# First experts' rows added to nodes in DRAM by accumulating scatters, in a GNN and MoE kernel on one core

## What is computed

```python
x = x + L0_gnn(layernorm(x), src, dst, ...)        # attention over edges
# L0_ffn: 8 experts, each node goes to its best 2; an expert takes 187 nodes
xf = layernorm(x)
probs = softmax(xf @ gate_w.T + gate_b)
topw, topi = top_k(probs, 2)
sel_w, sel_idx = top_k(wm.T, cap)                  # per expert: the nodes it takes, their weights
h = gelu(einsum('ecd,edh->ech', xf[sel_idx], w1) + b1)
out = einsum('ech,ehd->ecd', h, w2) + b2
of = zeros((T, D)).at[sel_idx].add(out * sel_w)
x = x + of
x = x + L1_gnn(layernorm(x), edge_attr_4, edge_attr_8, ...)   # messages, summed per node
x = x + L1_ffn(layernorm(x), ...)                  # two banks of 8 experts
```

## Time and profile before

| | us |
|---|---|
| median of three runs | 1875.65 (1869.82 to 1876.59) |
| the profiled execution | 1875.17 |
| its span, first to last instruction | 1873.40 |
| PE, DVE, ACT, POOL busy | 1594.3, 959.7, 701.4, 559.6 |
| first experts, first matmul of rows to last copy of a result | 867.23 to 1211.61 |
| opening of messages, first instruction to first gather | 1216.20 to 1267.03 |
| ACT's clear of 12 blocks | 1216.22 to 1221.54 |

### The profile page before, as it was taken

The page is one execution under the profiler, slowest core; times in us unless marked ns, Lnnn a source line. Parts: engine busy times, 40 slices in busy tenths (PEclk is TensorE's granted clock), DMA queues, the critical chain, the costliest instruction groups (busy, mean ns, idle before and its releaser), DMA issues. The chain is left out here.

```text
span 1873.4 us, 31644 instructions
## 1 busy us (share of the span) xinstructions
PE 1594.3 (85%) x9860; PEld 1167.9 (62%) x9860; DVE 959.7 (51%) x1950; ACT 701.4 (37%) x1610; POOL 559.6 (30%) x638
## 2 busy tenths in 40 slices
PE   1993077999999797897999999858999999898994
PEld 0551045888888455555999999844555555655662
DVE  8330098766766386361000000168999999542233
ACT  0230055555555133443211112154555555441331
POOL 6777601101010121151000000046555555133133
PEclk6997588999999898798999999968999999998997
DMA  9900011011000600557566552075555555619985
GB/s 290 312 11 6 6 43 23 13 23 22 12 11 1 149 12 1 220 142 249 198 229 238 218 196 99 18 216 165 156 158 158 156 156 150 215 37 287 353 268 183
DMA packets 131143, 252.87 MB, mean 135 GB/s; under 512 B 35344, under 2 KB 52596, under 8 KB 126572
## 3 DMA queue, kind: packets, MB, share of 16 engines
q1 hardware_dynamic: 91692, 171.81, 27.6%
q0 software_dynamic: 39360, 79.86, 14.6%
HBM read 196.03 MB, written 55.52 MB: 134 GB/s over the span
## 5 line engine op out<-in xcount | busy, mean ns | idle before, releaser
L1998 PE MATMUL acc<-prod,ohy 128*64 128x256 f32 x1056 | 249.1, 386 | 7.3 <-DVE prod L2116 7.3
L2042 ACT ACTIVATE ohy<-oh,RECS 128x64 f32<-128x64 f32 x704 | 187.0, 336 | 151.6 <-PE acc L1998 151.6
L1998 PEld LDWEIGHTS acc<-prod,ohy 128*64 128x64 f32 x1056 | 138.4, 138 | 131.9 <-issue 69.5
L1975 POOL DMA_INDIRECT rows<-up_dram,idx x176 | 167.0, 949 | 144.3 <-DVE prod L2116 101.2
L272 POOL DMA_INDIRECT rec_dram<-recs,pos x157 | 160.4, 1022 | 59.9 <-issue 48.9
L2001 PE MATMUL acc<-prod,ohy 128*64 128x256 f32 x704 | 177.3, 395 | 0.0
L1752 DVE TENSOR_SCALAR FT<-y_ps,b2T 128x188 f32<-128x188 f32 x32 | 13.2, 413 | 319.2 <-PE y_ps L1701 319.2
L1689 PE MATMUL hid_ps<-FT,W 128*128 128x188 f32 x1024 | 168.1, 326 | 0.7 <-ACT FT L1726 0.7
L2116 DVE TENSOR_TENSOR prod<-w_ps,rows 128x768 f32<-128x768 f32 x176 | 166.3, 945 | 0.0
L1689 PEld LDWEIGHTS hid_ps<-FT,W 128*128 128x128 f32 x1024 | 165.6, 192 | 0.9 <-issue 0.9
L1701 PE MATMUL y_ps<-hid,W 128*128 128x188 f32 x1024 | 164.5, 323 | 0.0
(11 more groups left out here) (380 smaller groups left out, 2638.2 us busy)
## 6 DMA issues: line engine op xcount, KB each, us to landing
W<-in_L_ffn_w SPq DMA_DIRECT2D x16, 4096.0 KB, 15.9
bankW_sp<-in_L_ffn_W_sp SPq DMA_DIRECT2D x2, 4096.0 KB, 23.9
xin<-zeros SPq DMA_DIRECT2D x31, 256.0 KB
h_dram<-h3e SPq DMA_DIRECT2D x22, 256.0 KB, 4.8
h<-h_dram SPq DMA_DIRECT2D x22, 256.0 KB
QF<-q_dram SPq DMA_DIRECT2D x20, 250.0 KB, 4.1
xin_sp<-zeros SPq DMA_DIRECT2D x17, 256.0 KB
xin_fq<-zeros SPq DMA_DIRECT2D x17, 256.0 KB
```

Of the source, the lines that this page charges most:

```text
L1975: pool.indirect_dma_start(out=rows[:, t, :], out_offset=None, in_=up_dram, in_offset=bass.IndirectOffsetOnAxis(ap=idx[:, par, t:t + 1], ax ...
L1998: upper = lambda m: nc.tensor.matmul(acc[0:HALFB, bank, :].rearrange("p (b c) -> p b c", c=MUL)[:, m:4:3 - m, :], ohs[:, 1 + m, :], pr[:, ...
L2042: last = nc.scalar.activation(ohy[:, t % OHY, i, :], oh[:, par, t, :], ACT.Copy, scale=RECS[:, bass.ds(BATCH * g + t, 1), 4 + i])
```

## The change

Every row that goes to an expert gets 8 more columns (EXTRA): its two weights, its two experts, and four times its node's number. A blank row carries zeros and a number past the 1250 nodes, a different one for each of 128 rows. X is stored to a new DRAM array, x_dense, during place_choices. Each expert's DVE part reads from its rows the node numbers (nodeI) and the weight that belongs to this expert, and weights the result as it copies it to ye. POOL then adds ye to the rows of x_dense by two scatters per expert, 94 rows each, in which the DMA adds to what stands there; each waits until the one before has landed. messages opens by loading X back from x_dense, tile by tile, on SP; gathers, additions, slot_out, yout0 and the wait before RECS are gone. POOL, not ACT, clears the 12 blocks of MSG. DVE's and POOL's loops over experts are written out.

```diff
+EXTRA = 8
+WIDE_ROW = DIM + EXTRA
...
-    xin0 = dram("xin0", (EXPERTS * ROWS0 + 2 * NODES, DIM))
-    yout0 = dram("yout0", (EXPERTS * ROWS0, DIM))
+    xin0 = dram("xin0", (EXPERTS * ROWS0 + 2 * NODES, WIDE_ROW))
+    x_dense = dram("x_dense", (NODES + 128, DIM))
...
+                        zeros_in += fill_zeros(sp, x_dense[NODES:NODES + 128, :], zeroed)
...
+                        nc.gpsimd.iota(zeros[:, DIM + 4:WIDE_ROW], pattern=[[0, 4]], base=NODES, channel_multiplier=1,
+                                       allow_small_or_imprecise_dtypes=True)
+                        nc.gpsimd.memset(zeros[:, 0:DIM + 4], 0.0).then_inc(consts, 1)
...
                         for b in range(ECHUNKS):
                             store_hidden(sp, b)
+                            if b < TILES:
+                                for p0, p1 in TILE_PARTS:
+                                    sp.dma_start(x_dense[P * b + p0:P * b + p1, :], X[p0:p1, b, :]).then_inc(x_stored, 16)
                         all_stored(sp)
+                        sp.wait_ge(x_stored, 32 * TILES)
...
+                        nc.gpsimd.iota(N[:, :, DIM + 4:WIDE_ROW], pattern=[[P, TILES], [0, 4]], base=0, channel_multiplier=1,
+                                       allow_small_or_imprecise_dtypes=True).then_inc(tagged, 1)
                         pool.wait_ge(bases_ready, 1)
+                        pool.wait_ge(tagged, 3)
...
+                        nc.vector.tensor_copy(N[:, :, DIM:DIM + 2], best[:, :, 0:2]).then_inc(tagged, 1)
+                        nc.vector.tensor_copy(N[:, :, DIM + 2:DIM + 4], idxF[:]).then_inc(tagged, 1)
...
-                        step(nc.vector.tensor_reduce(rank[:], parts[:], X_AXIS, ALU.add))
-                        step(nc.vector.tensor_scalar(keep[:], rank[:], CAP0 - 0.5, None, ALU.is_lt))
-                        step(nc.vector.scalar_tensor_tensor(out=rank[:], in0=idxF[:], scalar=float(ROWS0), in1=rank[:],
-                                                            op0=ALU.mult, op1=ALU.add))
-                        step(nc.vector.tensor_tensor(slot_out[:P], rank[:], keep[:], ALU.mult))
-                        step(nc.vector.tensor_tensor(weight[:], best[:, :, 0:2], keep[:], ALU.mult))
...
+                                sp.wait_ge(noted, 2 * (2 * r + b + 1))
+                                sp.sem_inc(tick, 1)
                                 load_rows(sp, 2 * r + 2 + b, b)
...
-                        last = EXPERTS - 1
-                        for c in range(2):
-                            sp.wait_ge(back_moved, 2 * last + c + 3)
-                            first = last * ROWS0 + HALF0 * c
-                            for p0, p1 in HALF0_PARTS:
-                                sp.dma_start(yout0[first + p0:first + p1, :], ye[last % 2][p0:p1, c, :]).then_inc(last_stored, 16)
-                        sp.wait_ge(last_stored, 64)

                     @block.gpsimd
                     def _(pool):
-                        def store(r, b):
-                            pool.wait_ge(back_moved, 2 * (2 * r + b + 1) + 2)
-                            pool.sem_inc(tick, 1)
-                            rows = yout0[bass.ds((2 * r + b) * ROWS0, ROWS0), :].rearrange("(c p) d -> p c d", p=HALF0)
-                            pool.dma_start(rows, ye[b][:]).then_inc(stored[b], 16)
-                            pool.wait_ge(stored[b], 16 * (r + 1))
-                            pool.sem_inc(y_free, 1)
-
-                        with pool.Fori(0, EXPERTS // 2 - 1) as r:
-                            for b in range(2):
-                                store(r, b)
-                        store(EXPERTS // 2 - 1, 0)
+                        for e in range(EXPERTS):
+                            b = e % 2
+                            pool.wait_ge(noted, 2 * (e + 1))
+                            for c in range(2):
+                                pool.wait_ge(back_moved, 2 * e + c + 3)
+                                if e + c >= 1:
+                                    pool.wait_ge(landed, 16 * (2 * e + c))
+                                pool.indirect_dma_start(
+                                    out=x_dense, out_offset=bass.IndirectOffsetOnAxis(ap=nodeI[:, e, c:c + 1], axis=0),
+                                    in_=ye[b][:, c, :], in_offset=None, compute_op=ALU.add).then_inc(landed, 16)
+                        pool.wait_ge(landed, 32 * EXPERTS)
...
-                                dve.wait_ge(y_free, e + 1)
-                                for c in range(2):
-                                    dve.wait_ge(back_done, 2 * e + c + 1)
-                                    nc.vector.tensor_copy(ye[b][:, c, :], turn_ps[:HALF0, c, :]).then_inc(back_moved, 1)
+                        for e in range(EXPERTS):
+                            r, b = divmod(e, 2)
+                            dve.wait_ge(x_loaded[b], 32 * (r + 1))
+                            nc.vector.tensor_copy(nodeI[:, e, :], xe[b][:, :, DIM + 4]).then_inc(noted, 1)
+                            for c in range(2):
+                                nc.vector.scalar_tensor_tensor(out=match[:, c, e, :], in0=xe[b][:, :, DIM + 2 + c], scalar=float(e),
+                                                               in1=xe[b][:, :, DIM + c], op0=ALU.is_equal, op1=ALU.mult
+                                                               ).then_inc(matched, 1)
+                            dve.wait_ge(matched, 2 * (e + 1))
+                            nc.vector.tensor_tensor(weight[:, e, :], match[:, 0, e, :], match[:, 1, e, :], ALU.add).then_inc(noted, 1)
+                            for d in range(KC):
+                                dve.wait_ge(y_done, KC * e + d + 1)
+                                nc.vector.tensor_scalar(yT[:, d, :], y_ps[:, d % 2, 0:ROWS0], b2T[:, e * KC + d:e * KC + d + 1],
+                                                        None, ALU.add).then_inc(y_moved, 1)
+                            dve.wait_ge(noted, 2 * (e + 1))
+                            if e >= 2:
+                                dve.wait_ge(landed, 32 * (e - 1))
+                            for c in range(2):
+                                dve.wait_ge(back_done, 2 * e + c + 1)
+                                nc.vector.tensor_scalar(ye[b][:, c, :], turn_ps[:HALF0, c, :], weight[:, e, c:c + 1], None, ALU.mult
+                                                        ).then_inc(back_moved, 1)
...
             def load(sp):
+                for t in range(TILES):
+                    if t == 2:
+                        load_mixer(sp)
+                    for p0, p1 in TILE_PARTS:
+                        sp.dma_start(X[p0:p1, t, :], x_dense[P * t + p0:P * t + p1, :]).then_inc(x_back[t], 16)
+
+            def load_mixer(sp):
...
-            def fetch(pool):
-                for n, (t, source, slots, _) in enumerate(jobs):
-                    if n >= RING:
-                        pool.wait_ge(added, n - RING + 1)
-                    pool.indirect_dma_start(
-                        out=got[:, n % RING, :], out_offset=None, in_=source,
-                        in_offset=bass.IndirectOffsetOnAxis(ap=slots(t), axis=0)).then_inc(arrived[n % RING], 16)
...
-                for n, (t, _, _, weight) in enumerate(jobs):
-                    dve.wait_ge(arrived[n % RING], 16 * (n // RING + 1))
-                    if n >= 1:
-                        dve.wait_ge(added, n)
-                    nc.vector.scalar_tensor_tensor(out=X[:, t, :], in0=got[:P, n % RING, :], scalar=weight(t),
-                                                   in1=X[:, t, :], op0=ALU.mult, op1=ALU.add).then_inc(added, 1)
-                    if n % per_tile == 0 and t >= 1:
+                for t in range(TILES):
+                    dve.wait_ge(x_back[t], 32)
+                    step(nc.vector.bn_stats(st6[:, t, :], X[:, t, :]))
+                    nc.vector.bn_aggr(mv[:, t, :], st6[:, t, :]).then_inc(stats_done, 1)
+                    if t >= 1:
                         scale(t - 1)
-                    if n % per_tile == per_tile - 1:
-                        dve.wait_ge(added, n + 1)
-                        step(nc.vector.bn_stats(st6[:, t, :], X[:, t, :]))
-                        nc.vector.bn_aggr(mv[:, t, :], st6[:, t, :]).then_inc(stats_done, 1)
-                        between(t)
+                    between(t)
...
                         load_mix(sp)
-                        first_added(sp)
...
+                        rest = MSG[:, CLEARED_BY_DVE + 4:, :]
+                        nc.gpsimd.memset(rest, 0.0).then_inc(cleared, 1)
                         pool.sem_inc(products, BATCH)
-                        fetch_rows(pool)
...
-                        rest = [128, BLOCKS - CLEARED_BY_DVE - 4, DIM]
-                        nc.scalar.activation(MSG[:, CLEARED_BY_DVE + 4:, :], zeros[:].unsqueeze(1).to_broadcast(rest), ACT.Copy
-                                             ).then_inc(cleared, 1)
```

(10 more changed lines are left out.)

52 lines of the change are left out of this document (15 added, 37 removed).

## The result

The changed kernel takes 1886.81 us (median of 5 runs, 1880.47 to 1889.68) beside 1875.65 before: a ratio of 1.0063, 95% interval 1.0045 to 1.0080, 11.2 us at the medians. Beside the kernel before on another chip it was 1.0069 (1.0044 to 1.0094). It is slower, by about the amount forecast, but the traces show that two terms of the sum were off in opposite directions, and that the agreement is in part luck.

The account below looks back on a forecast made before the run. A chain of stages with barriers, where only what follows the last expert and the messages opening counts: 17.8 - 6.6 + 0.3 = +11.5 us on 1875.17 gives 1886.7 us, range 1872 to 1897.

Parts of the forecast that it names:

- Front and placing: Before the experts: extra fill and wider rows covered by SP's wait; X stores and wider scatters add 0.3 us (0 to +2).
- Inside the experts: Between experts: extra DVE instructions, SP wait and two serial scatters, even at 15 us each, cost nothing, covered by PE's matmuls.
- Behind the last expert: From the last result to the next stage: two serial scatters on two DMA engines delay it 17.8 us (+4.2 to +27.6).
- the single scatter: After the last expert: one accumulating scatter takes 10.4 us, with 2.2 fixed; a plain write would take 6.7.
- rival 3: After the last expert: accumulating is dearer, 15.3 us per scatter, +21.3 in all, 1896.5 us; chance 0.13.
- rivals 1 and 2: Last scatters: accumulating costs only a write, 6.7 us each, 1879.3, chance 0.21; or they spread or overlap, 3.6, 1873.1, 0.14.
- My own signs for this part: After the last expert: scatters landing in 9 to 12 us, DMA share near 0.12, new stage 16 to 20 us later.
- Opening, first tile: Messages opening: first normalisation at S + 9.1 (S, the stage's start; S + 10.2 before), POOL's clear holding DVE's copy.
- Opening, cadence and tail: Messages opening: ten tiles in 25.6 us, then 9.5 to the first gather at S + 44.2, saving 6.6 us.
- The bound for a clock that is high from the fifth cycle on: Messages opening: with PE's clock high from the fifth cycle, the cadence takes 25.0 us and the tail 9.2.
- No wait for RECS: Messages opening, fifth tile: RECS arrives before DVE needs it; up to 3 us wait if loading takes as long as before.
- Rival 4: Messages opening gives little, -3 instead of -6.6 us, with clock low and DVE held for RECS: 1890.3 us; chance 0.10.

Follow-up runs that it names:

- e3: The kernel before with only the wide rows, the X stores and the fill of the dump rows added: 1872.07 us, ratio 0.9999.
- e2: The changed kernel with scatters that write the rows instead of adding them: 1878.11 us, ratio 1.0031.
- e4: The changed kernel with MSG's 12 blocks cleared by ACT again instead of POOL: 1887.82 us, ratio 1.0090.
- e6: The changed kernel with scatters of 96 partitions, and POOL waiting for DVE's copy of blocks_of before it clears MSG: 1869.17 us, one profiled execution.
- e11: The changed kernel again, unchanged, on a chip with a longer front: 1982.93 us, ratio 1.0069 to the kernel before there.
- e10: The kernel before again, unchanged, on a chip with a longer front: 1971.49 us, one execution.
- e8: The changed kernel with 96-partition scatters, RECS asked for before the sixth tile, and POOL clearing all of MSG after DVE's copy: 1870.04 us, ratio 0.9990.
- e9: The kernel of e8 with W4 loaded before the fifth tile, and RECS, W4 and first marks used two tiles later: 1967.59 us on the slower chip, ratio 0.9972.

## Why the prediction was right, and where it was not

*What bounds the kernel.* Right: only what stands behind the last expert and the opening moved.

*Front and placing.* +0.3 forecast, nothing measured: 10.0 against 9.9 us at the end of placing, and e3 the same as before within its interval (0.9981 to 1.0016).

*Inside the experts.* Right that it costs nothing. A scatter there lands after up to 22.3 us, median 16.6, above the 15 that I had allowed for, but the stretch is no longer than before (345.9 and 346.0 against 346.8 and 346.9).

*Behind the last expert.* The mechanism was right, the size not: +17.8 forecast, +24.6 measured (30.5 less 5.9). The engines were counted right, two of sixteen, and adding did make each transfer dearer by more than half. The term that was mis-sized is the single scatter, 10.4 taken and 13.2 measured. It came from a plain write of 6.7, which e2 has at 8.7, and an addition of 3.7, which is 4.5. The transfer itself was nearly met, 9 us (1206 to 1215) where I took 8.2, but not by its parts: the plain rows move at 32 GB/s and not at 42 to 52, and adding makes 9 of 6 us, which is less than double. The rest was missed around it. The 11.4 us of the store, and so the 2.2 us of fixed time that I took from it, hold POOL's issue of a plain store, 1.69; with the adding the issue is 2.55. And the first scatter lands 12.4 us after its issue, 0.8 before the next issue, where I had put 0.2. Some 0.4 us of each scatter I can't place. Two scatters make 5.6 us of the miss; the rest is in the first one's start and the barrier. What the small packets cost isn't shown. 13.2 lies between the forecast and rival 3 (15.3); rivals 1 and 2 are out. My own signs for this part were missed on the high side: 9 to 12 us to the landing, and a new stage 16 to 20 us later.

*Opening, first tile.* S + 9.1 forecast, S + 8.4 measured. The copy ended at S + 5.5, forecast S + 5.6, and e4 and e6 show that it is POOL's clear that holds it. It cost 1.9 us, and e6 gives these back in the first tile (S + 6.5).

*Opening, cadence and tail.* 25.6 and 9.5 forecast; 24.4 and 9.0, and on the second pair 25.3 and 9.1, measured. The bound for a clock that is high from the fifth cycle on was added up wrongly: 2 x 2.8 + 2 x 2.96 + 5 x 2.54 is 24.2, not 25.0, and the measured 24.4 lies just above it. "No wait for RECS" was wrong. In the first pair DVE waits 2.95 us and ACT feels 0.52 of it; in the second (e11) it is 4.0 and 1.54. This is why the nine steps take 0.9 longer in the second. Rival 4 is out: the opening gave more than forecast, not less. Together the opening gave 9.0 us in the first pair and 7.1 in the second, where 6.6 was forecast.

*The sum.* By its pieces the change should cost 24.6 - 9.0 = 15.6 us (24.5 - 7.1 = 17.4 in the second pair). The ratios say 11.8 (8.4 to 15.0), and 13.6 (8.7 to 18.5) on the slower chip; e4, with pieces that add up to 15.7, has 16.9 (11.2 to 22.3). So the forecast had the mechanism right, and that it met the measured time within a microsecond is luck: the scatters were priced 7 us too low, while the opening gave 2.4 more and the front took 0.3 less than forecast, and some 4 us that the pieces don't explain went the same way as these. Where these are is not settled: the experts began earlier in the changed kernel in both pairs (8.1 and 2.0 us), and from the first gather to the end it took 1.3 and 5.5 us less; among kernels with the changed front the experts' start varies from 855.4 to 863.0, and that last stretch, the same code in all, from 605.1 to 608.0 on the first chips, so one pair of executions proves little. But 611.0 on the last chip stands apart from 616.5 and 616.6: PE is busy 559.0 us in it instead of 562.8 in e10, at a mean granted clock of 0.97 instead of 0.96, and why isn't shown. And e3 alone shows no gain in front.

## What to carry to other kernels

Count the DMA engines of every store or scatter that stands alone on the path by the divisors of its partitions: 94, 95 and 96 rows took 13.2, 8.0 and 4.9 us here, and two rows of padding turned the change from 0.6% slower into no difference. Before you take a stall out of an opening, list the loads in the order in which they land: the 1.9 us won in front in e6 and a part of the 3.0 in e8 were given back at the next late load, until in e9 loads and uses were put in one order. Moving a clear to an idle engine is not free while it holds a copy on the engine that is late: here it held DVE's copy for 1.9 us.

## What the runs showed of the hardware

- A scatter of 94 rows that adds moves 22 to 23 GB/s on two engines, a plain one 32 to 50. POOL's issue of it is 2.55 us against 1.47, and with 96 rows 1.41 even with the adding.
- The pair of adding scatters made 1348 packets under 512 B with 94 rows, 450 with 95 and 32 with 96, for nearly the same rows; the pair that only writes made 704. With 94 rows 571 of the first scatter's 674 pass before 1207, ahead of nearly all rows. I can't say what they carry.
- A DVE copy of 176 columns begun under a POOL clear of 6144 columns takes 2.18 us and ends with it, against 0.25 when the clear is on ACT (e4) or behind the copy (e6).
- Beside the weight loads of the experts a scatter of 94 rows lands after 16.6 us in the median (12.4 to 22.3), against 12.6 alone.
